# Perceiver layer on one core: holding back the second pair's loads, and later weights, at the head

## The reference, cut to what matters

```python
x = x + xattn(layernorm(x), ctx_1024, ...)      # 128 queries, 12544 keys, 16 heads of 64
x = x + attn(layernorm(x), ...)                  # self-attention over 128 rows, LoRA weights
x = x + ffn(layernorm(x), weight, scale, bias)   # fp8-rounded linear layer

# inside xattn
lat = layernorm(latents, ln_l_w, ln_l_b); ctx = layernorm(context, ln_c_w, ln_c_b)
q = lat @ Wq;  k, v = split(ctx @ Wkv, 2)
attn = softmax(clip(einsum(q, k) * D ** -0.5, -11, 11))
out = einsum(attn, v) @ Wo + bo
```

## Time and profile before

| what | value |
| --- | --- |
| median of 3 runs | 1068.35 us (1067.48 to 1068.49) |
| the profiled execution: time, and its span | 1069.03 us, 1067.3 us |
| PE busy in the span | 1059.9 us (99%) |
| DVE, ACT, POOL busy | 933.8, 663.2, 177.5 us |
| bytes read from HBM | 58.20 MB |

### The profile page before, as it was taken

How to read it: one execution, slowest core, us unless ns; L and a number is a source line. 1 busy time by engine, 2 the same in 40 slices (tenths; PEclk the granted TensorE clock), 3 DMA queues, 4 the chain that set the end, 5 groups by cost and what they waited for, 6 DMA issues and landing times.

```text
span 1067.3 us, 18064 instructions
## 1 busy us (share of the span) xinstructions
PE 1059.9 (99%) x5501; PEld 901.8 (85%) x5501; DVE 933.8 (87%) x1329; ACT 663.2 (62%) x934; POOL 177.5 (17%) x213
## 2 busy tenths in 40 slices
PE   9999999999999999999999999999999999999998
PEld 7888888888888888888888888888888888888886
DVE  4999999999999999988898888888888888878885
ACT  4666666666666666656666666666666666665642
POOL 3233332332332333322000000000000000000000
PEclk9999999999999999999999999999999999999999
DMA  5312212212212212122151111111111111111000
GB/s 202 95 55 70 74 51 72 74 49 74 74 49 74 64 59 74 52 81 69 53 117 37 44 31 43 44 30 44 44 30 44 38 35 44 31 44 31 1 1 6
DMA packets 52925, 58.78 MB, mean 55 GB/s; under 512 B 31202, under 2 KB 33316, under 8 KB 52772
## 3 DMA queue, kind: packets, MB, share of 16 engines
q1 hardware_dynamic: 52468, 58.19, 18.3%
q10 hardware_dynamic: 432, 0.27, 0.1%
HBM read 58.20 MB, written 0.13 MB: 55 GB/s over the span
## 4 chain that ended last, share of the span: by engine, by line
PE 98%; DMA 1%; DVE 0%; SPq 0%; issue 0%; ACT 0%; DVEq 0%
PE wide L464 25%; PE wide L465 25%; PE wide L466 25%; PE wide L505 18%; DMA wq<-in_Wq_dram 1%; PE wide L527 1%; PE wide L541 1%; PE wide L556 1%; PE wide L562 0%; PE wide L549 0%; PE wide L522 0%; PE wide L764 0%; PE wide L534 0%; PE wide L515 0%; PE wide L747 0%; PE wide L694 0%
## 5 line engine op out<-in xcount | busy, mean ns | idle before, releaser
L836 ACT ACTIVATE ex<-wide,c_rstd 128x512 f32<-128x512 f32 x392 | 270.5, 690 | 221.9 <-PE wide L466 214.0
L464 PE MATMUL wide<-qk_hi,d_hi 128*128 128x512 f32 x784 | 310.8, 396 | 0.0
L465 PE MATMUL wide<-qk_lo,d_hi 128*128 128x512 f32 x784 | 307.4, 392 | 0.0
L466 PE MATMUL wide<-qk_hi,d_lo 128*128 128x512 f32 x784 | 305.3, 389 | 0.0
L1050 DVE TENSOR_TENSOR ph<-ex,ph 128x1024 fp32r<-128x1024 f32 x195 | 237.9, 1220 | 15.8 <-ACT ph L843 15.8
L1059 DVE TENSOR_TENSOR den_all<-den_all,ex 128x1024 f32<-128x1024 f32 x193 | 236.3, 1225 | 4.7
L505 PEld LDWEIGHTS wide<-ph,vhl 128*128 128x128 f32 x1568 | 213.8, 190 | 15.2
L505 PE MATMUL wide<-ph,vhl 128*128 128x256 f32 x1568 | 218.7, 282 | 0.0
L829 ACT ACTIVATE vhl<-wide,c_rstd 128x512 fp32r<-128x512 f32 x196 | 135.1, 689 | 131.2 <-PE wide L466 131.2
L843 ACT CAST ph<-ex 128x1024 fp32r<-128x1024 f32 x195 | 204.1, 1046 | 0.1
L1023 DVE TENSOR_SCALAR ex<-ex 128x1024 f32<-128x1024 f32 x195 | 135.3, 694 | 73.0 <-ACT ex L836 68.3
(11 more groups left out here) (163 smaller groups left out, 615.5 us busy)
## 6 DMA issues: line engine op xcount, KB each, us to landing
t_all<-in_ctxT_dram SPq DMA_DIRECT2D x98, 384.0 KB, 3.1
x_pair<-in_ctx_dram SPq DMA_DIRECT2D x49, 256.0 KB, 2.7
diff<-sig_all SPq DMA_DIRECT2D x194, 0.5 KB, 1.9
wkv<-in_Wo_dram SPq DMA_DIRECT2D x2, 1024.0 KB, 9.9
wq<-in_Wq_dram SPq DMA_DIRECT2D x2, 512.0 KB, 8.7
wkv<-in_Wv_dram SPq DMA_DIRECT2D x2, 512.0 KB, 6.8
wkv<-in_Wk_dram SPq DMA_DIRECT2D x1, 512.0 KB, 10.5
wkv<-in_Wk_dram SPq DMA_DIRECT2D x1, 256.0 KB, 3.2
```

The costliest lines, as they stand in the source:

```text
L464: pe.matmul(dst, hi, mhi, start=start, stop=False)
L465: pe.matmul(dst, hi, mlo, start=False, stop=False)
L466: return pe.matmul(dst, lo, mhi, start=False, stop=stop)
L836: act.activation(ex[b][:, c * HC:(c + 1) * HC, :], sc_bank[c][:, :].rearrange("p (h q) -> p h q", h=HC), ACT.Exp, scale=c_rstd[s4][:, b:b ...
```

## The change

Two waits are added in the list of SP ahead of the loads for pair 1, and one ahead of the second query weights. No load is added, removed or put in another order.

```diff
             sp.dma_start(x_pair[0][:, :, :], ctx[0, :, :, :]).then_inc(s_xin[0], 16)
             sp.dma_start(wq[:, 0, :, :], Wq[:, 0, :, :]).then_inc(s_wq[0], 16)
             sp.dma_start(t_pair[0], ctxT[0, :, :, :]).then_inc(s_tin[0], 16)
+            sp.wait_ge(s_wkc, 16)
+            sp.wait_ge(s_xin[0], 16)
             load_rows(1, 1)
             load_columns(1, 1)
+            sp.wait_ge(s_wq[0], 16)
             sp.dma_start(wq[:, 1, :, :], Wq[:, 1, :, :]).then_inc(s_wq[1], 16)
             sp.dma_start(wkv[:, 1, 0, :, :], Wv[:, 0, :, :]).then_inc(s_wv[0], 16)
             for n in range(2, SLOTS):
```

## The result

The changed kernel takes 1069.63 us at the median of 21 runs (1068.31 to 1071.98), the kernel before 1068.57 us at the median of 21 in the same comparison. The ratio, which leaves out one slow run of the kernel before at 2149.46 us, is 1.0013 with a 95% interval from 1.0007 to 1.0019. The medians are 1.06 us apart, and the ratio stands for 1.4 us, 0.7 to 2.0 us by its interval. The forecast was 1068.05 us in a range up to 1069.5, a small gain. The direction was wrong, and the median lies 0.13 us above the range.

What follows compares the result with a forecast made beforehand. PE bounds the kernel, with the first query weights the one load on its path. -0.3 us for them, 0 for pair 1, second query weights and issues: 1068.7 us profiled, 1068.05 at the median, range 1066.8 to 1069.5.

Steps and rivals of the forecast that it cites:

- The bound: At the head, the first query weights are the one load on PE's path; their landing moves the whole kernel, down to 9.57 us.
- Lagging engines: DMA engines each work in order, some ahead of others; a load waits for the slowest; gain for first query weights 0.3 us.
- holding back others then gives nothing: At the head, a weight load alone is as slow as one among others, so the gain from below is 0.
- Rival A: Held-back loads did take memory from the first query weights; PE starts at 9.6 to 10.2 us, time 1066.8 to 1067.5; chance 0.26.
- The third wait at 0: Wait ahead of the second query weights costs 0: issued at 11.1 us, they land at 14.9, wanted at 15.13.
- stand in the same line and move with the first: Second query weights, with 0.2 us to spare, queue in the first ones' line and move with them.
- rival B: Second query weights land late, at 15.5 to 16.7 us, costing 0.4 to 1.6 us; chance 0.17, later than that 0.04.
- The range: 1066.8 to 1069.5 us, taking in A from its low end and B; both ends of the third wait's price said to stay inside.
- The signs: New trace: PE's first-query-weights wait 1.0 to 1.5 us, line 330 over 7.3, line 549 runs within 4.1, first rows at 8.4.
- Pair 1 at 0: First two waits, ahead of pair 1's loads, cost 0, up to about 1 us if its columns came at 15.8 us.
- SP's later work at 0: SP's seven loads behind the third wait end by 14.4 to 16.7 us; sigma row up to 1.7 us late, cost 0.

Runs made afterwards that it cites:

- e5: Kernel before with one added wait, for the first query weights, ahead of the value weights and all that follows: 1068.32 us, ratio 1.0000.
- f14_queue_long: Kernel before with 14 unused matmuls ahead of PE's second-query-weights wait; pair 2's loads, then a wait for first query weights, precede the second's load: 1070.80 us.
- e8: Kernel before with each half of the query, key and value weights laid out by itself in HBM: 1067.08 us, ratio 0.9984.
- e2: Changed kernel without its first two waits, so only the second query weights and what follows are held: 1070.53 us, ratio 1.0017.
- e7: Changed kernel with each half of the query, key and value weights laid out by itself in HBM: 1068.67 us, ratio 1.0002.
- e4: Changed kernel with 14 added matmuls (filler, result unused) on PE ahead of its wait for the second query weights: 1070.78 us.
- f14_before: Kernel before with 14 added matmuls (filler, result unused) on PE ahead of its wait for the second query weights: 1071.79 us.

## Why the prediction was wrong, point by point

- **The bound.** Right: the first query weights were the one load on the path, PE was free at about 9.6 us, and all that followed moved as a block. Every microsecond of the second queries' start is one of the time (15.37 to 16.86 us is 1.49, from 1069.22 to 1070.63 us in the profiled executions is 1.41).
- **Lagging engines.** The landing in order of issue was no more than half of the story. The step "holding back others then gives nothing", from the rate of line 344's load alone, failed: the held loads did hold up the first query weights, by 1.0 us at the median where I took 0.3. Rival A, which had the cause as the bytes of all held loads, is nearer, but e5 and f14_queue_long put it on the second query weights, and e8 on how the weights lie in HBM.
- **The third wait at 0.** This is the step that turned the sign: "+ 0 (second query weights)" measured 1.6 us of idle time in the profiled execution and 2.1 us at the median. I let the second query weights "stand in the same line and move with the first", with 1.3 us for their bytes at full rate. Held, they took 5.71 us from issue, with the engines at 20 GB/s each at 12 to 14 us. I had 4.4 us for the load alone and a landing at 16.7 us as the upper end, so rival B had the mechanism; it landed at 15.33 us. What I missed is that B and A come together. The first queries' early start moves up the moment at which PE wants the second ones, from 15.13 to 13.70 us, so that a landing only 0.5 us later than before is an idle time of 1.61 us. I gave A and B as alternatives, each with its own chance, where one brings on the other.
- **The range.** I wrote that both ends of the third wait's price stay in it. They don't: B's own price ran to 1069.9 us, and the range ended at 1069.5. The median of 1069.63 us lies in B's bracket and outside the range.
- **The signs.** They spoke for A and B at once. PE no longer waited for the first query weights (A: under 0.6 us), line 330 took 6.3 us to landing (A: 6.3 or less), and the second run of line 549 started 5.7 us after the first (B: over 4.1). The second query weights landed 5.7 us after the first, over the 4 us at which the forecast was to fail. The first rows landed at 7.2 us, neither at 8.4 as forecast nor at the 6 us that would have settled the cause.
- **The clock.** Not in the forecast at all. I priced PE's wait by its length. Behind waits of 2.12 us (e2) and 2.06 us (e7) another 1.56 us were lost at half clock (about as much in e7); behind the 1.61 us of the changed kernel's profiled execution none were. The fall accounts for the six runs at 1071.35 us and above, but not for the median.
- **Pair 1 at 0.** Right. DVE took pair 1's columns at 12.89 us, where it was 13.76, and PE did not wait for it.
- **SP's later work at 0.** Right: seven loads issued from 9.62 to 14.19 us (4.6 us; 3.3 to 5.55 foreseen), the sigma row at 14.29. The value weights and second key weights were not waited for:

```profile
21.00 3.59 PE L544 MATMUL wide<-wkv,foldT 128*128 128x512 f32 x8
24.43 1.89 PE L537 MATMUL wide<-foldT,wkv 128*128 128x256 f32 x8
```

The sum with measured terms: -1.0 us for the first queries (1070.78 - 1071.79, with filler), and for the wait the changed kernel's median above what e4 would take without its filler, 1069.63 - (1070.78 - 3.23) = +2.1 us. Together that is +1.1, against 1.06 us measured. The second term is taken from the measured median itself, so the agreement tests only that f14_before less its filler (1068.56 us) is the kernel before (1068.57). A test of the second term by itself is the profiled execution: 1069.22 - 1067.55 = 1.67 us, and in its trace the second queries start 1.67 us later than PE could have begun them. The clock has no share in either.

## What to carry to other kernels

Before a wait is put ahead of a load, set the load's whole time from issue to landing (here 5.7 to 6.7 us for 512 KB) against the work that its first reader has left, counted from the new, earlier start: if the wait does its job, that work begins sooner and the slack shrinks by as much. A load issued early can hide all of that time (in the kernel before it was 9.7 us, and PE did not wait); hold back only what nobody wants soon, as in e5, and expect little from that. Where one load seems to crowd another, try how the data lies in HBM before the order of issue; and where a change lets TensorE wait longer, look at the granted clock behind the wait and at the spread of the runs, not at its length alone. No run here shows from what length on the clock falls.

## What was not expected of the hardware

- At 12 to 14 us each DMA engine went at 20 GB/s in the changed kernel and at 18 in e7, where little stood ahead of the held weights, and at 25 in the kernel before and 24 in f14_queue_long, where more did.
- Rows of 4 KB at an 8 KB pitch, for all three weights, cost 1.4 us at the head against the same rows one behind the other (1068.5 to 1067.08 us), with the same bytes (5.4 MB in the first 30 us of both).
- In e2 the granted clock fell about 1 us after PE had taken up its work again (idle to 15.84 us, clock at 0.50 from 16.8 us), in e7 0.6 us after (15.34 and 15.9 us), and the half clock then lasted for 3.4 us of full work in both.
